# Layer 0's maxima over pairs of keys: first score plus relu of the difference

## The reference, cut to what matters

```python
scores = jnp.einsum('bhqd,bhkd->bhqk', q, k) / jnp.sqrt(jnp.float32(D_K))
attn = jax.nn.softmax(scores, axis=-1)                    # layer 0, 1601 keys
...
top_scores, top_idx = jax.lax.top_k(scores, eff_k)        # layer 1, eff_k = 32
w = jax.nn.softmax(top_scores, axis=-1)
```

## Time and profile before

| | |
|---|---|
| median of 3 runs | 5038.38 us (5035.5 to 5039.1) |
| profiled execution, its own time | 5038.72 us |
| its span, first to last instruction | 5036.8 us |
| busy: TensorE matmuls, VectorE, ScalarE, GpSimd | 85%, 85%, 80%, 23% of the span |
| mean busy share of the DMA engines' time, queue q1 | 27.2% |

### The profile page before, as it was taken

The page is one execution under the profiler, slowest core; times in us unless marked ns, Lnnn a source line. Parts: engine busy times, 40 slices in busy tenths (PEclk is TensorE's granted clock), DMA queues, the critical chain, the costliest instruction groups (busy, mean ns, idle before and its releaser), DMA issues. The chain is left out here.

```text
span 5036.8 us, 108348 instructions
## 1 busy us (share of the span) xinstructions
PE 4299.9 (85%) x33333; PEld 2098.9 (42%) x33862; DVE 4269.4 (85%) x22968; ACT 4019.8 (80%) x5260; POOL 1157.3 (23%) x2649
## 2 busy tenths in 40 slices
PE   5879779999797999879889998987999799988775
PEld 2435235353443535344343534444353344534222
DVE  5478998988989898998989899898989989888782
ACT  2558769889697898879789898987989698898774
POOL 3122112222122222212222222222222122121111
PEclk8989989999998999999999999999999999999887
DMA  5332322323133232323323232331323233131110
GB/s 131 75 85 60 70 56 64 81 65 73 48 77 76 54 77 64 75 59 76 71 53 77 71 79 62 75 80 49 78 65 78 57 76 76 36 70 39 31 28 21
DMA packets 356926, 332.13 MB, mean 66 GB/s; under 512 B 102659, under 2 KB 313750, under 8 KB 356310
## 3 DMA queue, kind: packets, MB, share of 16 engines
q1 hardware_dynamic: 356310, 324.86, 27.2%
HBM read 217.55 MB, written 107.13 MB: 64 GB/s over the span
## 5 line engine op out<-in xcount | busy, mean ns | idle before, releaser
L988 DVE MAX8 cand<-s 128x8 f32<-128x67 f32 (+1 forms) x12288 | 1981.1, 221 | 119.7 <-DVEq L1131 71.3
L959 ACT ACTIVATE prob<-wide 128x1024 f32<-128x1024 f32 (+1 forms) x1792 | 1776.4, 1025 | 195.4 <-PE wide L654 86.1
L1074 DVE TENSOR_REDUCE part<-score 128x1 f32<-128x512 f32 x1536 | 1012.4, 678 | 198.0 <-PE score L608 86.2
L654 PE MATMUL wide<-q,k_att 128*128 128x256 bf16 (+1 forms) x6656 | 1017.0, 278 | 159.4 <-ACT s L940 64.2
L940 ACT ACTIVATE s<-wide 128x1024 f32<-128x1024 f32 (+1 forms) x1024 | 837.9, 841 | 283.4 <-DVEq L1131 197.2
L700 PE MATMUL att<-prob,v 128*9 128x256 f32 (+1 forms) x14336 | 1046.6, 383 | 12.1 <-ACT prob L959 6.0
L949 ACT ACTIVATE below<-wide 128x1024 bf16<-128x1024 f32 (+1 forms) x832 | 818.5, 1026 | 131.1 <-PE wide L654 126.9
L654 PEld LDWEIGHTS wide<-q,k_att 128*128 128x128 bf16 (+1 forms) x6656 | 560.4, 100 | 615.9 <-ACT s L940 218.8
L1315 POOL TENSOR_SCALAR flag<-cand,ends 128x24 bf16<-128x24 f32 x512 | 179.8, 351 | 2060.0 <-DVE ends L1013 1782.9
L608 PE MATMUL score<-k_scan,q 128*128 128x512 bf16 x1298 | 498.3, 398 | 81.6 <-DVE part L1074 32.9
L676 PE MATMUL wide<-below,minus_ident 128*128 128x512 bf16 (+1 forms) x1556 | 482.3, 388 | 92.7 <-ACT below L949 70.0
(11 more groups left out here) (167 smaller groups left out, 4881.5 us busy)
## 6 DMA issues: line engine op xcount, KB each, us to landing
k_scan<-k_stack SPq DMA_DIRECT2D x512, 150.1 KB, 3.3
k_stack<-split_b SPq DMA_DIRECT2D x576, 128.0 KB, 2.6
k_att<-k_stack SPq DMA_DIRECT2D x384, 192.0 KB, 3.4
ctxT<-in_ctx_dram SPq DMA_DIRECT2D x32, 800.5 KB, 5.0
q_stack<-split_b SPq DMA_DIRECT2D x192, 64.0 KB, 2.0
q<-q_stack SPq DMA_DIRECT2D x128, 96.0 KB
self_stack<-split_b SPq DMA_DIRECT2D x192, 64.0 KB, 2.0
k_self<-self_stack SPq DMA_DIRECT2D x64, 96.0 KB
```

What stands on the lines that cost most here:

```text
L654: r = tensor.matmul(ps[0:kc, j * S:(j + 1) * S], m.k_att[kn % 3][:, j, c0:c0 + kc], rows[:, j, :], start=(j % 2 == 0), stop=(l == 0), skip ...
L959: scalar.activation(pr[0:kc, :], ps[0:kc, :], ACT.Exp, scale=SCALE).then_inc(sem["wide_done"], 1)
L988: i = vector.max(cand[:, :, c], s[:, KCUT[c]:KCUT[c + 1]])
L1074: vector.tensor_reduce(m.part[:, QT * hh + qt, c:c + 1], score[i % 2][:, :], AX.X, ALU.max).then_inc(sem["score_max"], 1)
```

## The change

Layer 0's maxima are found over pairs of keys. The keys are cut into a first half (keys 0 to 800) and a second half (keys 800 to 1600). Of two keys a and b, max(a, b) = a + relu(b - a). TensorE makes the first scores a (`n0_a`, 801 columns) and the differences b - a (`n0_d`, 801 columns, one matmul over both halves: the tile of keys now holds the second half in rows 0 to 47 and the first half in rows 64 to 111, against a query tile whose rows 64 to 111 hold the negated queries). ScalarE takes the relu of the differences into SBUF (`n0_relu`), and VectorE adds the two and keeps the greatest in one instruction (`n0_max`). `n0_all` is gone. A group has 8 such units.

- `n0_a` and `z_score` share one PSUM buffer `score` of two banks in place of two of one bank; `n0_d` takes turns in `wide`, where ScalarE drains it.
- `z_score` and `z_max` take two heads at a time: 128 steps of 1024 columns for 256 of 512.
- GpSimd negates the split queries of layer 0 (one more instruction in `split.w_q`), six more DMAs a sequence store them (`minus_out`), and `q_in.0` loads them in a second DMA; a key tile of layer 0 (`k_scan.0`) comes in three DMAs of 801 columns in place of one of 1601.
- `mx[0]` has two buffers, the `fold` of the relu two.
- The lists of all engines but GpSimd are new. Per sequence, `n0_max` stands 32 times for 112, `z_max` 8 for 16, `n0_relu` 32 times; the `rank`, `check`, `cut`, `exp` and `c1` words keep their numbers, and their lags move by at most two.

```diff
+HALF = (NK + 1) // 2
...
-        score = [psum(f"score{n}", BANK) for n in range(2)]
+        score = psum("score", 2 * BANK)
...
+                    elif name in ("n0_a", "n0_d"):
+                        g, n = key
+                        hh, qt = divmod(n, QT)
+                        kn = HG * g + hh
+                        if name == "n0_a":
+                            ps, a0, i = score, 0, turn("score", name, *key)
+                            if i:
+                                q.wait_ge(sem["score_max"], i)
                         else:
-                            for qt in range(QT):
-                                r = tensor.matmul(score[i % 2][:, qt * REST:(qt + 1) * REST],
-                                                  rows[:, hh, qt * P:(qt + 1) * P], keys[:, BANKS * BANK:],
-                                                  start=True, stop=True)
-                        r.then_inc(sem["score_full"], 1)
+                            ps, a0 = fill(name, *key), HALF
...
+                        for x in range(0, HALF, BANK):
+                            x1 = min(x + BANK, HALF)
+                            r = tensor.matmul(ps[:, x:x1], m.q[0][g % QBUF[0]][:, hh, qt * P:(qt + 1) * P],
+                                              m.k_scan[0][kn % 2][:, a0 + x:a0 + x1], start=True, stop=True)
...
+                    elif name == "n0_relu":
+                        ps, n = full("n0_d", *key), turn("fold", name, *key)
+                        if n >= 2:
+                            q.wait_ge(sem["score_max"], after("n0_max", (n - 2) // (HG * QT), (n - 2) % (HG * QT)))
+                        scalar.activation(m.fold[n % 2][:, :], ps[:, 0:HALF], ACT.Relu).then_inc(sem["wide_done"], 1)
...
-                        if n < SCANS - 1:
-                            qt, c = divmod(n, BANKS)
-                            vector.tensor_reduce(m.part[:, QT * hh + qt, c:c + 1], score[i % 2][:, :], AX.X,
-                                                 ALU.max).then_inc(sem["score_max"], 1)
...
+                        vector.tensor_tensor_reduce(out=r[:, :], in0=score[:, 0:HALF], in1=r[:, :], scale=1.0, scalar=NEG,
+                                                    op0=ALU.add, op1=ALU.max,
+                                                    accum_out=m.mx[0][g % 2][:, n:n + 1]).then_inc(sem["score_max"], 1)
...
+                            gpsimd.tensor_scalar(m.q_minus[:, :, :], part[:, :, 0:S], -1.0, None,
+                                                 ALU.mult).then_inc(negated, 1)
...
+                    elif name == "minus_out":
+                        b, = key
+                        q.wait_ge(negated, b + 1)
+                        for k in range(NT):
+                            sync.dma_start(d.q_minus[b, k, :, :, :].rearrange("j h s -> h j s"),
+                                           m.q_minus[:, QPART[k], :]).then_inc(minus_out, 16)
...
+                        if l == 0:
+                            for r0, c0, s0 in ((0, 0, 0), (0, HALF, NK - HALF), (64, HALF, 0)):
+                                sync.dma_start(m.k_scan[0][kn % 2][r0:r0 + ROWS, c0:c0 + HALF],
+                                               keys[:, s0:s0 + HALF]).then_inc(k_scan_in[0][kn % 2], 16)
```

More of the change, by code:

```diff
@@ L74 @@
     ln_stats=("normed", 1), ln_aggr=("normed", 2), ln_scale=("normed", 1), n0_max=("score_max", 1),
-    z_max=("score_max", 1), n0_all=("n0_ready", 1), check=("checked", 2), least=("least_done", 5),
+    z_max=("score_max", 1), check=("checked", 2), least=("least_done", 5),
     o_norm=("o_done", 2), x_add=("x_done", 1), route_best=("routed", 4), route_pick=("routed", 6),
@@ L90 @@
[L90 to L99, removed]
@@ L127 @@
-    dve="""
[L128 to L144, removed]
@@ new lines @@
+        cut_add n0_a cut_add pv_z u_turn.0 c1 n0_d n0_a s_1*2 pv.1 cut_add flag cut_add pv.1 c1 z_score c1 s_1*2
+        pv.1 cut_add u_turn.2 cut_add row_turn.2 c1 n0_d pv.1 c1 s_1*2 pv.1 cut_add row_turn.0 n0_a cut_add n0_d
+        pv.1 s_1*2 pv.1 cut_add n0_a cut_add flag pv.1 c1 w_k.1 c1 s_1*2 pv.1 cut_add*2 n0_a n0_d pv.1 c1 s_1 pv.1*2
+        cut_add s_z n0_d flag s_z n0_a c1 pv.1 s_0 n0_d pv_z*2 s_0 u_turn.1 w_k.1 c1 pv.0 c1 u_turn.2 s_0*2
+        row_turn.1 pv.0 c1 pv.0 s_0 n0_a s_0 pv.0 s_0 pv.0 c1 n0_a s_0*2 pv.0*2 n0_d pv.0 s_0*2 pv.0 flag s_0 c1
@@ L180 @@
+        "mix_start.z": 3, "n0_relu": 22},
     dve={
-        "rank": 310, "n0_max": 72, "n0_all": 3, "check": 40, "o_norm.1": 12, "least": 10, "x_add.1": 3,
-        "ln_stats.z": 3, "ln_aggr.z": 3, "ln_scale.z": 3, "o_norm.0": 4, "route_best.z": 3, "x_add.0": 1,
-        "ln_stats.v": 1, "route_pick.z": 3, "ln_aggr.v": 1, "ln_scale.v": 1, "z_add": 6, "route_best.v": 1,
-        "z_max": 60, "route_pick.v": 1, "v_add": 14, "ln_stats.w": 0, "ln_aggr.w": 0, "ln_scale.w": 0, "x_add.v": 2,
-        "ln_stats.u": 2, "ln_aggr.u": 2, "ln_scale.u": 2, "o_norm.2": 16, "x_add.z": 4},
+        "rank": 308, "check": 40, "o_norm.1": 12, "least": 10, "x_add.1": 3, "ln_stats.z": 3, "ln_aggr.z": 3,
@@ L256, in streams @@
             of(f"{name}.{l}", name, [(l, g) for g in groups])
-    for name in ("n0", "n0_max"):
-        of(name, name, [(g, hh, n) for g in groups for hh in range(HG) for n in range(SCANS)])
+    for name in ("n0_a", "n0_d", "n0_relu", "n0_max"):
+        of(name, name, [(g, n) for g in groups for n in range(HG * QT)])
     for name in ("c1", "c1_out"):
@@ L264, in streams @@
         of(name, name, [(g, hh) for g in groups for hh in range(HG)])
-    for name in ("n0_all", "least", "kq_in"):
+    of("minus_out", "minus_out", [(b,) for b in batches])
+    for name in ("least", "kq_in"):
         of(name, name, [(g,) for g in groups])
     for name in ("z_score", "z_max"):
-        of(name, name, [(g, h) for g in groups for h in range(HG)])
+        of(name, name, [(g, n) for g in groups for n in range(HG // 2)])
     for name in ("s_z", "exp_z", "pv_z"):
@@ L340, in build @@
     after, before, turn = T.after, T.before, T.turn
-    T.number("pe", "wide", ("w_k", "w_v", "w_q", "u_q", "z_qk", "v_w1", "z_moe", "c1", "s_z", "s_0", "s_1"))
+    T.number("pe", "wide", ("w_k", "w_v", "w_q", "u_q", "z_qk", "v_w1", "z_moe", "c1", "n0_d", "s_z",
+                              "s_0", "s_1"))
     drains = T.number("act", "wide_out", ("w_k_out", "w_v_out", "w_q_out", "u_q_out", "z_qk_out", "v_gelu", "z_moe_out",
-                                          "c1_out", "exp_z", "exp_0", "exp_1"))
+                                          "c1_out", "n0_relu", "exp_z", "exp_0", "exp_1"))
     DRAIN = dict(w_k="w_k_out", w_v="w_v_out", w_q="w_q_out", u_q="u_q_out", z_qk="z_qk_out", v_w1="v_gelu",
-                 z_moe="z_moe_out", c1="c1_out", s_z="exp_z", s_0="exp_0", s_1="exp_1")
+                 z_moe="z_moe_out", c1="c1_out", n0_d="n0_relu", s_z="exp_z", s_0="exp_0", s_1="exp_1")
     assert [(DRAIN[name], key) for name, key in T.rings["wide"]] == drains
-    T.number("pe", "score", ("n0", "z_score"))
+    T.number("pe", "score", ("n0_a", "z_score"))
     T.number("dve", "score_out", ("n0_max", "z_max"))
-    assert [(dict(n0="n0_max", z_score="z_max")[n], k) for n, k in T.rings["score"]] == list(T.rings["score_out"])
+    T.number("act", "fold", ("n0_relu",))
+    assert [(dict(n0_a="n0_max", z_score="z_max")[n], k) for n, k in T.rings["score"]] == list(T.rings["score_out"])
     weighings = T.number("pe", "pv", ("pv_z", "pv"))
@@ L451, in build @@
         ctx_in, x_out = semaphore("ctx_in"), semaphore("x_out")
+        negated, minus_out = semaphore("q_negated"), semaphore("q_minus_out")
         split_out = [semaphore(f"split_out{n}") for n in range(2)]
@@ L635, in _ @@
                         if l == 0:
-                            q.wait_ge(sem["n0_ready"], after("n0_all", g))
+                            q.wait_ge(sem["score_max"], after("n0_max", g, HG * QT - 1))
                         elif l == 1:
```

233 lines of the change are left out of this document (124 added, 109 removed), and 4 rows, old and new, of the table sp.

## The result

The changed kernel takes **5184.69 us** (median of four runs, 5180.33 to 5185.34), beside 5036.94 for the kernel before in the same series (four runs, 5029.44 to 5039.1). The ratio is 1.0294 with a 95% interval of 1.0276 to 1.0312: 148 us slower, where 58 us faster was forecast.

A forecast was written before the change was run, and what follows sets the result against it. VectorE was taken as the bound, at 92.7% of a 285.3 us sequence, then ScalarE at that share: 2.6 us less over 13 sequences (34) plus 24 for rescans, 58 off 5038.72, gave 4980 us, range 4900 to 5040.

The forecast's parts named there:

- TensorE's columns: TensorE streams 51,232 columns a sequence before and 51,264 after, in 72 steps for 128; counted 0.
- SP's issues: SP issues 42 more DMAs a sequence, 26 us of 285; key tiles are loaded two heads ahead, so counted 0.
- the rescans: `check` may come earlier against ScalarE's waiting `c1_out`: 3 us for each of 8 whole-row search phases, 24 us less.
- the 32 turns of `wide`: Extra fills and drains a sequence on the two `wide` buffers between TensorE and ScalarE; left to the second rival.
- the same share: ScalarE as the new bound fills 92.7% of a sequence, as VectorE did: 282.7 us, 2.6 less a sequence.
- 262.1: ScalarE's floor in us a sequence after the change: 238.5 with all overlaps won, plus 23.6 for the 32 relus.
- Rival 2: Two `wide` buffers: ScalarE's 34.4 us of waits stay beside the floor, 296.5 a sequence, 5185 us; chance 0.27.
- The sign set for this rival: ScalarE's waits without rescans over 23 us a sequence, on `wide`, would show the two-buffer rival.
- Rival 1: ScalarE's waits go with VectorE's load: 273 us a sequence, 4855 us with the rescans; chance 0.17.
- V: The theory that VectorE set the pace before the change, with its 264 us of a sequence.
- rival 3: TensorE, 92% busy and not relieved, is the bound already: a sequence stays at 285, 5030 us; chance 0.08.
- rival 4: VectorE's new instruction runs at half rate: 25.6 us more a sequence on VectorE, about 285, 5035 us; chance 0.06.

The follow-up runs named there:

- e6: The changed kernel with the differences' matmul and relu both cut from 801 to 16 columns, the turn kept: 5125.70 us, 1.0179 of the kernel before.
- e7: The kernel before with layer-0 reductions over 64 and their score matmuls over 256 of 512 columns: 4920.77 us, 0.9772 of the kernel before.
- e9: The changed kernel without the score matmuls of layers 0 and 2 (VectorE reads zeros), two `wide` buffers kept: 5156.64 us, 1.0234 of the kernel before.
- e2: The kernel before with VectorE's layer-0 reductions cut from 512 to 64 columns: 4946.47 us, 0.9825 of the kernel before.
- e1: The changed kernel with each relu cut from 801 to 16 columns, all turns and matmuls kept: 5138.09 us, 1.0206 of the kernel before.
- e11: The kernel before without the score matmuls of layers 0 and 2 (VectorE reduces zeros), two `wide` buffers kept: 4982.55 us, 0.9893 of the kernel before.
- e12: The kernel before without the score matmuls of layers 0 and 2, their two banks made a third `wide` buffer: 4899.52 us, 0.9728 of the kernel before.
- e10: The changed kernel without the score matmuls of layers 0 and 2, their two banks made a third `wide` buffer: 4944.91 us, 0.9813 of the kernel before.
- e5: The changed kernel without the matmul and relu of the differences (VectorE adds zeros): 4951.00 us, 0.9832 of the kernel before.
- e3: The kernel before with 32 more 801-column relus a sequence, read from `wide` buffers that ScalarE drains anyway: 5263.23 us, 1.0454 of the kernel before.

## Why the prediction was wrong

- *The durations were right.* `n0_max` took 0.98 us and 0.08 for reading its maximum, where 1.02 was forecast, `z_max` 1.22 for 1.21, the relu 0.846 for 0.842. VectorE, reckoned as before, has 30.6 us a sequence less (31.0 forecast), ScalarE 21.2 more (23.6).
- *Counted at 0, rightly:* TensorE's columns (taking columns away gave 12 to 28 us in `e6`, `e7` and `e9`), the single `score` buffer, and SP's issues (TensorE waits for no key tile of `k_scan`). Of the rescans, a wait fell from 21.3 to 20.3 us each, not by 3, which makes 8 us in place of 24.
- *Counted at 0, wrongly:* the 32 turns of `wide`. **This is the step that failed**: the sum left them to a rival, took ScalarE's own time as the bound, and gave it "the same share" as VectorE. The runs show 175 us for these turns with next to no work in them, and of the change's 174 us without scores 129 that go with a third buffer. The two inputs of that step are off as well. VectorE was not the bound alone (`e2`: relieved of 40 us, the kernel gives back 6). And 262.1, a floor that took every overlap as won, was not reached: busy time came to 272.1, with 22.7 of waits on top. That 272.1 is 92.3% of 294.8, so that the share comes out as forecast, is chance: with relus of 16 columns (`e1`) a sequence takes 293.4 and ScalarE is busy for 86.6% of it.
- *Rival 2* has the place and the sign, and its 5185 the measured number, but partly by luck: it let 34.4 of waits stand over a floor of 262.1 (296.5; measured 294.8) and charged 13 sequences where 15.6 paid. Its argument against, that a fill need only be shorter than a drain, leaves out that the fill waits for the drain before last, so that two hand-overs and TensorE's other work must fit into one drain's time as well. Behind most empty relus of `e6` they did not; behind the full relus they mostly did, and the relu's own time is paid instead. The sign set for this rival (waits over 23) was not met: 22.7.
- *Rival 1* fell with V, rival 3 with `e7` and `e9`, rival 4 with the 982 ns. Against rival 1 the prediction gave TensorE's waits on VectorE as 43.9 us; that is one row, and those on `score` alone add up to 185. So that argument was weaker than it stood.

The Perfetto Trace Analysis page of the Trainium skill (section Optimization Strategy) says that a gap repeating on the engine that should be full can mean too little SBUF or PSUM for the next tile. The 83 and 212 us of the third buffer agree. Only a part of ScalarE's waits on `wide` was that gap: with the third buffer they fell from 336 to 292 us (`e11`, `e12`) and from 242 to 157 (`e9`, `e10`).

In this order of steps, from the kernel before to the changed one, the differences are -90 (VectorE's reductions, `e2`), -26 (half of the score columns, `e7`), +30 (lists, one score buffer, key loads, VectorE's new instructions, `e5`), **+175 (the turns, `e6`)**, +12 (their columns, `e1`) and +47 (the relu's length). Each step starts where the one before ended, so that they add up to +148 proves nothing; another order would give other sizes.

## What to carry to other kernels

Where two engines hand tiles to each other through two buffers, count the turns and not only the work in them: one more turn of next to nothing cost 0.35 us under one order of work and 0.75 under another, and 0.84 us more in a drain that was there already cost 0.45 (`e3`). Before work is moved off the engine with the highest busy share, shorten that work on a copy: if a large relief gives back little, as 40 us gave 6 here, another bound stands right behind it. A floor made from every possible overlap, divided by the share at which another engine stood, is no forecast: at nearly the same time a sequence, ScalarE's share was 92% with full relus and 87% with short ones.

## What the runs showed of the hardware

The instruction of VectorE that adds two inputs and keeps the maximum (`tensor_tensor_reduce`) is followed in the trace by a second one, 82 ns, that reads the maximum out. With both float32 inputs in SBUF (`e10`) the first takes 991 ns, hardly more than with one in PSUM (982), so no half rate shows there either. The profile lists it as a custom instruction; `SCALAR_TENSOR_TENSOR` with a kept maximum ran in no kernel here.

```profile
L1080 DVE CUSTOM_DVE_ANT_0 fold<-none,fold 128x801 f32<-128x801 f32 x416 | 412.3, 991 | 51.9 <-ACT fold L948 39.4 <-DVEq L1125 9.7 <-ACT prob L966 1.6
```
